# Output mixing on four row groups, with a signal per half of four pictures and corrections read by 16 transfers a wave

## Chip, cores and metric

The kernel runs on one core of a Trainium2 chip. The metric is the time on the device in microseconds (us). The kernel before took 838.54 us, the median of three runs (838.18 to 841.1).

## What is computed

The input is a batch of 32 pictures with 64 channels and 32 x 32 pixels. A first part (group normalization, windowed attention and a feed-forward layer) gives a new `x`. A second part, the one this case is about, adds a correction to it:

```python
# scores of 16 blocks of 8x8 positions, softmax, the 6 best positions, their features, then a small MLP
h = jax.nn.relu(feat @ W1 + b1)
rec = (h @ W2 + b2).reshape(NB, n, OC, LH, LW)
grid = rec.reshape(LRF, LRF, n, OC, LH, LW).transpose(2, 3, 0, 4, 1, 5)
grid = grid.reshape(n, OC, H, W)
return jnp.einsum('bohw,co->bchw', grid, out_w)
...
x = x + _L1_conv_ref(_gn(x), ...)
```

There are NB = 16 blocks of 64 positions in a picture, n = 32 pictures and OC = 7 reduced channels. So `rec` holds 512 rows (block and picture) of 7 x 64 = 448 numbers. The last line, the output mixing, turns the 7 reduced channels of each pixel into 64 channels by a 64 x 7 matrix, and the result is added to `x`. All numbers are float32.

## The kernel before

SBUF holds the pictures as 16 pairs: partitions 0 to 63 are the channels of picture p, partitions 64 to 127 those of picture 16 + p, and a pair has 1024 pixels in its free dimension. `xs` is the normalized `x` (its space is free once the features are picked), `x1` is the `x` to which the correction is added. Everything here happens in the last stage of the program. Each engine has a list of instructions written out by hand, and semaphores set the order between them.

The steps of the tail, with their lines:

- L1592: TensorE computes the second layer of the MLP for four tiles of 128 rows, in the order 0, 2, 1, 3 (`ROW_TILES`), into banks 4 to 7 of PSUM. L1490: VectorE adds the bias of each and writes `rec`, in SBUF.
- L1407: SP, whose queue issues the transfers, stores each tile of `rec` to a scratch tensor in DRAM. The trip through DRAM turns rows of blocks and pictures into rows of channels.
- L1414: after every second tile (tiles 0 and 2 are the first eight pairs of both image halves, tiles 1 and 3 the last eight), SP waits until both stores have landed and issues two reads. Read a (for the pictures of half a) fills the 7 partitions from 7a on: 14 partitions in all, 8 pairs x 1024 pixels each, in runs of 64 numbers. This is called a wave here; there are two waves, h = 0 and 1.
- L1601: TensorE mixes. For each pair and each half of its pixels (512, one bank of PSUM) it waits until the bank is free and forms two products of 256 columns. The weights `ow` are 128 x 128: rows 0 to 6 hold the mixing matrix for the picture of partitions 0 to 63, rows 7 to 13 the one for the other picture, and the other 114 rows are zero. Only banks 0 and 1 are used. Each product runs as two passes in float32.
- L1496: VectorE adds the bank (128 x 512) to `x1` and signals. There are 32 such adds.
- L1422: SP waits for both adds of a pair and issues two stores of 64 partitions x 4 KB each to the output, 32 in all.
- L1324: earlier, one stage before, SP loads the weights of this stage, `ow` with two loads.

Order and waits: TensorE's half of a pair waits for the add of the same half of the pair before; VectorE waits for each half's products; SP issues the stores of `rec`, the reads and the output stores in this order in one queue. ACT's queue has no transfers in this stage, and ScalarE's last work in it is the first layer's activation (L1531). `after(eng, sem, count)` is a wait that is left out where the count is not positive.

## Time and profile before

| | us |
|---|---|
| median of three runs | 838.54 |
| profiled execution, its whole time | 839.52 |
| span of that execution, first to last instruction | 837.7 |
| TensorE matmul busy in the span | 718.8 |
| VectorE busy in the span | 518.8 |
| last matmul of the MLP to the end of the span, about | 51 |

The span is the stretch that the traces show; what lies outside it (839.52 - 837.7 = 1.8 us) is not broken down. Busy time of an engine counts its instructions only, not its waits. The changed part is the last 51 us or so: from 787 us, when TensorE finishes the MLP, to 837.7 us, when the last store has landed. In tables by stage, the granted clock is given as a share of TensorE's 2.4 GHz, so 1.00 is 2.4 GHz and 0.50 is 1.2 GHz. The DMA share is the mean busy share of 16 DMA engines by the times of their packets; packets can overlap, so it can pass 1.

### The profile page before, as it was taken

The page shows a single profiled execution, that of the slowest core. Times are in us where ns is not written, and L with a number is a line of the kernel's source. Part 1 is how long each engine was busy: PE and PEld are TensorE (multiplying, and loading weights), DVE is VectorE, ACT ScalarE, POOL GpSimd, SP SyncE. Part 2 cuts the span into 40 slices and gives each one's busy share as a digit, 9 for nine tenths or more (in the row PEclk, how much of TensorE's full clock was granted, in tenths as well). Part 3 has the DMA queues.
Part 4 walks back from the last instruction along what each step waited for, and adds up shares of the span by engine and source line. Part 5 has one row for each costly group of instructions (what it writes and reads, how often), then busy time and mean ns, then how long its engine had stood idle before and what let it go on. Part 6 is the DMA issues. An engine that isn't in the chain of part 4 may idle for free. (4 is left out here: it accounts for less than half of the span.)

```text
span 837.7 us, 21571 instructions
## 1 busy us (share of the span) xinstructions
PE 718.8 (86%) x8482; PEld 385.6 (46%) x8482; DVE 518.8 (62%) x964; ACT 488.4 (58%) x986; POOL 373.9 (45%) x464
## 2 busy tenths in 40 slices
PE   4784799999999999999998489999999648659587
PEld 3562455555555555555554132333333228644264
DVE  4791367767776676777776112777777857661155
ACT  3663366777777777777775368877777117733000
POOL 4696356677767677667766220022222233300000
PEclk9775599999999999999999879999999758969889
DMA  9630000000000000000000020221111212000478
GB/s 211 149 87 11 1 2 2 2 3 2 2 2 3 2 3 3 2 2 2 3 2 3 0 51 1 49 50 46 45 43 49 76 43 54 0 1 1 57 165 268
DMA packets 15436, 31.38 MB, mean 37 GB/s; under 512 B 7208, under 2 KB 9004, under 8 KB 15340
## 3 DMA queue, kind: packets, MB, share of 16 engines
q1 hardware_dynamic: 14216, 29.61, 14.5%
q8 instruction: 66, 1.08, 0.6%
q10 hardware_dynamic: 856, 0.20, 0.2%
q0 software_dynamic: 272, 0.27, 0.2%
q14 instruction: 26, 0.21, 0.1%
HBM read 20.70 MB, written 9.37 MB: 36 GB/s over the span
## 5 line engine op out<-in xcount | busy, mean ns | idle before, releaser
L757 POOL TENSOR_TENSOR sc<-sc,mx 128x512 f32<-128x512 f32 x128 | 133.6, 1044 | 34.2 <-DVE mx L705 34.2
L702 DVE TENSOR_TENSOR sc<-s_ps,bias_tab 128x512 f32<-128x512 f32 x128 | 87.7, 685 | 58.9 <-PE s_ps L532 58.9
L655 ACT ACTIVATE pt<-t_ps 128x512 f32<-128x512 f32 x128 | 75.9, 593 | 52.6 <-PE t_ps L543 51.4
L1199 POOL TENSOR_TENSOR square<-xs 128x1024 f32<-128x1024 f32 x16 | 33.8, 2110 | 162.2 <-DVE xs L1101 162.2
L705 DVE TENSOR_REDUCE mx<-sc 128x8 f32<-128x512 f32 x128 | 87.8, 686 | 4.4
L1018 ACT ACTIVATE hs<-h_ps,fb1s 128x512 f32<-128x512 f32 x128 | 78.1, 688 | 17.6 <-PE h_ps L932 17.5
L543 PEld LDWEIGHTS t_ps<-consts,sc 128*128 128x128 f32 x512 | 53.7, 141 | 73.1 <-issue 45.8
L543 PE MATMUL t_ps<-consts,sc 128*128 128x128 f32 x512 | 83.9, 286 | 2.2 <-ACT pt L655 1.6
L532 PE MATMUL s_ps<-kx,qu 32*64 32x128 f32 x2048 | 71.4, 276 | 1.5 <-DVE sc L702 1.4
L932 PE MATMUL h_ps<-xs,fw 64*128 64x512 f32 x256 | 68.4, 648 | 1.0 <-ACT hs L1018 1.0
L945 PE MATMUL c_ps<-hs,fw 128*64 128x512 f32 x256 | 62.0, 604 | 0.8 <-DVE fcsq L1045 0.7
L532 PEld LDWEIGHTS s_ps<-kx,qu 32*64 32x64 f32 x2048 | 56.0, 133 | 13.8 <-issue 12.0
L646 ACT ACTIVATE vd<-a_ps 64x256 f32<-64x256 f32 x128 | 48.2, 377 | 18.4 <-PE a_ps L485 17.3
L742 POOL TENSOR_TENSOR q_sq<-q_sb 128x512 f32<-128x512 f32 x32 | 33.2, 1039 | 48.7 <-ACT q_sb L622 48.7
L713 DVE TENSOR_TENSOR kx<-a_ps,k_sb 128x512 f32<-128x512 f32 x64 | 40.9, 681 | 22.4 <-PE b_ps L509 21.4
L728 DVE TENSOR_TENSOR ob<-b_ps,rsum 128x512 f32<-128x512 f32 x32 | 22.1, 692 | 48.3 <-ACT rsum L664 48.3
L1045 DVE SCALAR_TENSOR_TENSOR fcsq<-c_ps,fb,fcc 128x512 f32<-128x512 f32 x32 | 23.8, 745 | 39.7 <-ACT fcc L1027 39.7
L764 POOL TENSOR_TENSOR cc<-xs,cc 128x512 f32<-128x512 f32 x32 | 40.7, 1275 | 13.9 <-DVE cc L734 13.9
L145 POOL TENSOR_TENSOR xs<-raw,gn_rstd_sb 128x96 f32<-128x96 f32 (+1 forms) x144 | 37.6, 306 | 18.7 <-ACT bias_ps L198 10.7
L742 POOL TENSOR_TENSOR k_sq<-k_sb 128x512 f32<-128x512 f32 x32 | 33.2, 1040 | 25.9 <-ACT k_sb L615 25.9
L1601 PE MATMUL bank<-xs,ow 128*128 (+1 forms) x128 | 34.6, 417 | 11.0 <-DMA xs<-rec_scratch 11.0
L749 POOL TENSOR_TENSOR csq<-cc 128x512 f32<-128x512 f32 x32 | 33.3, 1039 | 20.7 <-ACT cc L671 20.7
(190 smaller groups left out, 1393.2 us busy)
## 6 DMA issues: line engine op xcount, KB each, us to landing
raw<-in_x_dram SPq DMA_DIRECT2D x32, 256.0 KB, 5.1
xr<-in_x_dram SPq DMA_DIRECT2D x32, 256.0 KB, 4.1
out_dram<-x SPq DMA_DIRECT2D x32, 256.0 KB, 3.8
rec_scratch<-r SPq DMA_DIRECT2D x4, 224.0 KB, 4.5
xs<-rec_scratch SPq DMA_DIRECT2D x4, 224.0 KB
w<-in_L_conv_W_dram SPq DMA_DIRECT2D x1, 784.0 KB
w<-in_L_conv_W_dram SPq DMA_DIRECT2D x1, 672.0 KB
consts<-in_c_consts_dram SPq DMA_DIRECT2D x1, 400.0 KB, 4.0
```

The lines of the kernel that those rows point to most:

```text
L532: last = pe.matmul(s_ps[j][TOK * w:TOK * (w + 1), 2 * i + m], qu[p % 2][a][row, at], kx[p % 2][a][row, :, at], start=True, stop=True)
L543: last = pe.transpose(t_ps[:, m], sc[n % KEPT][:, m].rearrange("c h k -> c (h k)"), ident)
L646: last = act.activation(to[to_lo:to_hi, :, w, :, DH * h:DH * (h + 1)], v[lo:hi, :, :, h], ACT.Copy)
L655: act.activation(pt[a][2 * hp + j][:, :, :], t_ps[:, :, :], ACT.Exp).then_inc(s["exped"], 1)
L702: dve.tensor_tensor(sc[n % KEPT][:, :, :, :], s_ps[j][:, :, :, :], bias_tab[:, j, hp], ALU.add)\
L705: dve.tensor_reduce(mx[n % KEPT][:, :], sc[n % KEPT][:, :, :, :].rearrange("c m h k -> c (m h) k"), X, ALU.max).then_inc(s["row_max"], 1)
L713: dve.tensor_tensor(kx[p % 2][a][:, h], a_ps[a][:, :], k_sb[a][:, :], ALU.mult)\
L742: pool.tensor_tensor(dst[a][:, :], src[a][:, :], src[a][:, :], ALU.mult).then_inc(s[done], 1)
L757: pool.tensor_tensor(v, v, mx[n % KEPT][:, :].unsqueeze(2).broadcast_to([128, 8, TOK]), ALU.subtract)\
L932: last = pe.matmul(h_ps[2 * half + a][:, :], fw1[lo:hi, a, half], xu[lo:hi, u], start=True, stop=True)
L945: last = pe.matmul(c_ps[lo:hi, :], fw2[:, m // 2], hs[:, u % 2, m], start=(m < 2), stop=(m >= 2))
L1018: act.activation(hs[:, u % 2, m], h_ps[m][:, :], ACT.Gelu, bias=fb1s[:, m // 2:m // 2 + 1])\
```

## The change

The mixing is laid over the four groups of 32 rows of the TensorE array. Pair p = 4k + q uses row group q: its 14 rows of corrections lie at partitions 32q to 32q + 13, in slot k of a `grid` that now has four slots of 1024 pixels for each row group (the first four pair slots of `xs`). `ow` gets a copy of the mixing matrix in each group. A call of `mix(k, half)` forms eight products, for four pairs and two quarters of 256 columns, with q innermost, so neighbouring products have different row groups and different banks; all eight banks are used, bank 2q + half for half a picture pair. It signals once for the eight products, and VectorE makes four adds behind each signal. A pair is stored after its second half, so SP waits for add number 8(p // 4) + p % 4 + 5. The reads of a wave become 16 transfers, eight (image half 0) from SP and eight (image half 1) from ACT, each for one q and one k. TensorE additionally waits until VectorE has read banks 4 to 7 (`rec`). The loops of the mixing, the adds and the stores are written out.

```diff
--- before.py
+++ after.py
@@ -1264,7 +1264,8 @@
                       (w2[:, :, :], mlp_w2.rearrange("(m k) n -> k m n", k=MT)), (mb[:, :], mlp_b1),
                       (mb2r[:, :], mlp_b2.rearrange("(a n) -> a n", a=1).broadcast_to([128, OUTDIM]))]
         for a, (lo, hi) in enumerate(HALVES):
-            tail_loads += [(w1s[lo:hi, :], mlp_w1[TOP * C:INDIM]), (ow[OC * a:OC * (a + 1), lo:hi], out_w)]
+            tail_loads += [(w1s[lo:hi, :], mlp_w1[TOP * C:INDIM])]
+            tail_loads += [(ow[32 * q + OC * a:32 * q + OC * (a + 1), lo:hi], out_w) for q in range(4)]
 
         with ExitStack() as stage:
             s = {k: sem(stage, "y_" + k) for k in
@@ -1376,7 +1377,7 @@
 
             rec = r[:, :, :, :].rearrange("c t n x -> c (t n x)")[:, 0:4 * OUTDIM].rearrange("c (t n) -> c t n", t=4)
 
-            grid = yt.rearrange("o p g n -> o p (g n)")
+            grid = xs[:, 0:4]
             psb = [ps(stage, f"bank{k}", [128, COLS]) for k in range(8)]
             ROW_TILES = (0, 2, 1, 3)
 
@@ -1398,6 +1399,17 @@
                                 src[:, :, :, :, q, a])
                 return last
 
+            def spread_rec(eng, h, a):
+
+                eng.wait_ge(rec_out[h], 32)
+                rows = rec_dram[256 * a + 128 * h:256 * a + 128 * (h + 1)]
+                for q in range(4):
+                    first = 32 * q + OC * a
+                    src = rows.rearrange("(k q g) (o l) -> q o k g l", k=2, q=4, l=TOK)[q]
+                    dst = grid[first:first + OC, 2 * h:2 * h + 2].rearrange("o k (g l) -> o k g l", l=TOK)
+                    for k in range(2):
+                        eng.dma_start(dst[:, k], src[:, k]).then_inc(rec_in[h], 16)
+
             with nc.Block() as block:
                 @block.sync
                 def _(sp):
@@ -1405,23 +1417,15 @@
                     for i, t in enumerate(ROW_TILES):
                         sp.wait_ge(s["rec"], i + 1)
                         sp.dma_start(rec_dram[128 * t:128 * (t + 1), :], rec[:, t]).then_inc(rec_out[i // 2], 16)
-                        if i % 2 == 0:
-                            continue
-                        h = i // 2
-                        sp.wait_ge(rec_out[h], 32)
-                        for a in range(2):
-                            rows = slice(256 * a + 128 * h, 256 * a + 128 * (h + 1))
-                            sp.dma_start(grid[OC * a:OC * (a + 1), 8 * h:8 * (h + 1)]
-                                         .rearrange("o p (g l) -> o (p g) l", l=TOK),
-                                         rec_dram[rows].rearrange("r (o l) -> o r l", l=TOK)).then_inc(rec_in[h], 16)
+                        if i % 2 == 1:
+                            spread_rec(sp, i // 2, 0)
                     out_pairs = out.rearrange("(a p) c h w -> a c p (h w)", a=2)
 
                     def store(p):
-                        sp.wait_ge(s["added"], 2 * p + 2)
+                        sp.wait_ge(s["added"], 8 * (p // 4) + p % 4 + 5)
                         for a, (lo, hi) in enumerate(HALVES):
                             sp.dma_start(out_pairs[a, :, p], x1[lo:hi, p]).then_inc(s["stored"], 16)
-                    store(0)
-                    with sp.Fori(1, PAIRS) as p:
+                    for p in range(PAIRS):
                         store(p)
                     sp.wait_ge(s["stored"], 32 * PAIRS)
 
@@ -1489,16 +1493,12 @@
                         dve.wait_ge(s["rec_ps"], i + 1)
                         dve.tensor_tensor(rec[:, t], psb[4 + i][:, 0:OUTDIM], mb2r[:, :], ALU.add).then_inc(s["rec"], 1)
 
-                    def add(p):
+                    for k in range(4):
                         for half in range(2):
-                            dve.wait_ge(s["mixed"], 2 * p + half + 1)
-                            v = x1[:, p, COLS * half:COLS * (half + 1)]
-                            dve.tensor_tensor(v, v, psb[half][:, :], ALU.add).then_inc(s["added"], 1)
-                    add(0)
-                    add(1)
-                    with dve.Fori(1, PAIRS // 2) as i:
-                        add(2 * i)
-                        add(2 * i + 1)
+                            dve.wait_ge(s["mixed"], 2 * k + half + 1)
+                            for q in range(4):
+                                v = x1[:, 4 * k + q, COLS * half:COLS * (half + 1)]
+                                dve.tensor_tensor(v, v, psb[2 * q + half][:, :], ALU.add).then_inc(s["added"], 1)
 
                 @block.scalar
                 def _(act):
@@ -1529,6 +1529,8 @@
                     for m in range(4):
                         act.wait_ge(s["hid_ps"], m + 1)
                         act.activation(hid[:, m], psb[m][0:MT, :], ACT.Relu, bias=mb[:, m:m + 1]).then_inc(s["hid"], 1)
+                    for h in range(2):
+                        spread_rec(act, h, 1)
 
                 @block.tensor
                 def _(pe):
@@ -1593,21 +1595,21 @@
                                              start=(m == 0), stop=(m == 3))
                         last.then_inc(s["rec_ps"], 1)
 
-                    def mix(p):
+                    def mix(k, half):
+                        after(pe, s["added"], 8 * (k - 1) + 4 * (half + 1))
+                        for y in range(2):
+                            for q in range(4):
+                                rows = slice(32 * q, 32 * q + 2 * OC)
+                                blk = grid[rows, k].rearrange("o (y x h w) -> o y h x w", y=4, x=4, h=8)[:, 2 * half + y]
+                                last = pe.matmul(psb[2 * q + half][:, 256 * y:256 * (y + 1)], ow[rows, :], blk,
+                                                 start=True, stop=True)
+                        last.then_inc(s["mixed"], 1)
+                    pe.wait_ge(s["rec"], len(ROW_TILES))
+                    for k in range(4):
+                        if k % 2 == 0:
+                            pe.wait_ge(rec_in[k // 2], 256)
                         for half in range(2):
-                            after(pe, s["added"], 2 * p - 1 + half)
-                            for y in range(2):
-                                blk = grid[:, p].rearrange("o (y x h w) -> o y h x w", y=4, x=4, h=8)[:, 2 * half + y]
-                                last = pe.matmul(psb[half][:, 256 * y:256 * (y + 1)], ow[:, :], blk,
-                                                 start=True, stop=True)
-                            last.then_inc(s["mixed"], 1)
-                    for h in range(2):
-                        pe.wait_ge(rec_in[h], 32)
-                        mix(8 * h)
-                        mix(8 * h + 1)
-                        with pe.Fori(4 * h + 1, 4 * (h + 1)) as i:
-                            mix(2 * i)
-                            mix(2 * i + 1)
+                            mix(k, half)
 
 
 N_PICK = 13
```

## Rows read from the trace of the kernel before

**Rows 1.** Chain that ended last, 770 to 838 us: start, length, what.

```profile
781.67 1.94 DMA rec_scratch<-r
...
783.97 13.96 DMA xs<-rec_scratch
...
797.97 34.63 PE bank L1601 x128
...
832.74 0.69 DVE x L1496
```

**Rows 2.** Who waited for whom, same stretch: total us, times, longest.

```profile
PE bank L1601 <- DMA xs<-rec_scratch: 11.0, 1, 11.0
```

**Rows 3.** VectorE: the adds as a group, first add, two adjoining instructions elsewhere.

```profile
L1496 DVE TENSOR_TENSOR x<-x,bank 128x512 f32 (+1 forms) x32 | 22.0, 687 | 23.8 <-PE bank L1601 23.8
...
800.08 0.69 DVE L1496 TENSOR_TENSOR x<-x,bank 128x512 f32<-128x512 f32 x1 [12.43 <-PE bank L1601]
...
518.77 0.75 DVE L1045 SCALAR_TENSOR_TENSOR fcsq<-c_ps,fb,fcc 128x512 f32<-128x512 f32 x1 [2.61 <-ACT fcc L1027]
519.44 0.74 DVE L1061 SCALAR_TENSOR_TENSOR fcc<-fcc,b,xs 128x512 f32<-128x512 f32 x1
```

**Rows 4.** Stages: length, busy of five engines (x count), PEclk, DMA share, GB/s.

```profile
784.50:785.50 1.00, 1.00 (x4) 0.55 (x3) 0.15 (x1) 0.00 (x0) 0.00 (x0) 1.00 0.32 75
785.50:791.50 6.00, 1.49 (x4) 0.40 (x3) 0.62 (x1) 0.00 (x0) 0.00 (x0) 0.96 0.63 34
...
793.00:796.50 3.50, 0.00 (x0) 0.00 (x0) 0.00 (x0) 0.00 (x0) 0.00 (x0) 0.50 0.66 47
...
799.50:800.50 1.00, 1.00 (x4) 0.81 (x3) 0.42 (x1) 0.00 (x0) 0.00 (x0) 0.50 0.44 98
800.50:805.00 4.50, 4.50 (x18) 3.23 (x18) 2.78 (x5) 0.00 (x0) 0.00 (x0) 0.92 0.62 39
805.00:812.00 7.00, 7.00 (x28) 4.42 (x27) 4.47 (x8) 0.00 (x0) 0.00 (x0) 1.00 1.07 191
812.00:824.00 12.00, 12.00 (x48) 7.84 (x46) 8.10 (x12) 0.00 (x0) 0.00 (x0) 1.00 0.92 334
824.00:832.00 8.00, 8.00 (x32) 5.23 (x31) 5.10 (x9) 0.00 (x0) 0.00 (x0) 1.00 0.86 249
```

**Rows 5.** Packets of the stretch 775 to 838 us, and its transfers by name.

```profile
DMA packets 6749, 10.24 MB, mean 163 GB/s; under 512 B 4188, under 2 KB 4700, under 8 KB 6748
...
out_dram<-x SPq DMA_DIRECT2D x32, 256.0 KB, 3.8
rec_scratch<-r SPq DMA_DIRECT2D x4, 224.0 KB, 4.5
xs<-rec_scratch SPq DMA_DIRECT2D x4, 224.0 KB
```

**Rows 6.** TensorE at 199 us: start, busy, products on four row groups.

```profile
199.32 0.70 PE L507 MATMUL a_ps<-rn,spread_keys 32*128 32x512 f32 x2 [0.31 <-ACT rn L635]
199.34 0.70 PE L509 MATMUL b_ps<-rn,consts 32*128 32x512 f32 x2
199.86 0.59 PE L507 MATMUL a_ps<-rn,spread_keys 32*128 32x512 f32 x2
199.87 0.59 PE L509 MATMUL b_ps<-rn,consts 32*128 32x512 f32 x2
```

**Rows 7.** Issue on SP: ns min/median/max, first and last start; a held issue; the second wave.

```profile
L1414 SPq DMA_DIRECT2D xs<-rec_scratch x4: 292/630/1052, 783.6 to 798.9; - x4
...
L1422 SPq DMA_DIRECT2D out_dram<-x x32: 494/495/2362, 802.3 to 834.3; - x32
...
784.97 6.37 SPq L1407 DMA_DIRECT2D rec_scratch<-r  x1
...
798.54 1.39 SPq L1414 DMA_DIRECT2D xs<-rec_scratch  x2
```

**Rows 8.** Loads of the mixing weights, and VectorE's first instruction of the stage.

```profile
L1324 SPq DMA_DIRECT2D ow<-in_L_conv_out_w_dram x2: 479/507/535, 689.9 to 691.0; - x2
...
727.93 0.59 DVE L1438 COPY scores_sb<-raw_scores 64x256 f32<-64x256 f32 x2 [3.19 <-PEq L1319]
```

## The prediction: what the change does to the time

> **What bounds the kernel now.** I read the chain of waits of the last stretch first, then who waited for whom, then the timeline of the queues, and last the busy time and the transfer rate by stage. The chain [rows 1] shows two long pieces after the second layer of the MLP. From 783.97 to 797.93 us nothing computes: TensorE waits 11.0 us for the corrections to come back from DRAM [rows 2]. From 797.97 the 128 matmul passes of the output mixing (64 products, two passes each) run 34.63 us to 832.60, and one add and the last store close the span at 837.7. So two things hold the tail: how long the first wave of read-back takes, and TensorE's pace in the mixing, 34.63/16 = 2.16 us a picture pair.
>
> Two resources lie close beneath TensorE. VectorE's 32 adds take 22.0 us in all [rows 3], about two thirds of the mixing. The transfers are nearer. The reader should look at the last two columns of the stage table [rows 4]: share of the 16 DMA engines and GB/s. The reads of corrections move 75 and 98 GB/s in their first microsecond, and then only 34, 47 and 39 GB/s, although the share stays above 0.6. From 812 to 824 us the stores run at 334 GB/s, and only from 824 at 249, which is TensorE's pace (a pair is 524 KB; 524/2.16 = 243). The time between is a backlog being worked off.
>
> Why reads are so slow can be half read from packet counts. Each read takes 256-byte runs (64 floats); four reads are 4 x 7 x 128 = 3584 packets. The stretch has 4188 packets under 512 bytes [rows 5]. The 604 left over are completions: 32 stores x 16, 4 stores of `rec` x 16 and 4 reads x 7 make 604 exactly. So a read runs on 7 of the 16 engines, as it has 7 channel rows outermost, and the other 9 do none of it. Each new transfer has 7 rows outermost too, so I count on 7 again. The Trainium skill has a rule for this in "DMA: Bandwidth & Descriptors" (Why a DMA increments its semaphore by 16 and not by 1): the slowest dimension of the two patterns sets the number of engines, and the trace agrees with its 604.
>
> In the fast first microsecond 7 engines at 75 to 98 GB/s do a run in 256 x 7/98 to 256 x 7/75 = 18 to 24 ns each; later at 34 to 47 GB/s one in 38 to 53 ns. So an engine can take runs twice as fast as it mostly does, and something behind it holds it. What the trace does not show is what.
>
> **Part by part.** *The mixing on four row groups.* A product now has 14 rows of weights at partition 32q, and neighbours lie on different groups and write different banks. The trace has that very pattern in another stage: four products of 512 columns on row groups 0 to 3 (the two of L507, the two of L509), two passes each, start at 199.32 and end at 200.46 us [rows 6]: 1.14 us for all four. One call of the new `mix(k, half)` has four groups with 2 x 256 columns each, the same columns, so 1.14 us at full clock instead of 4 x 1.08 us. At half clock I take 2.11 us, the time from the first pass at 797.97 [rows 1] to the first add at 800.08 [rows 3], where two 256-column products ran one after the other at clock 0.50 [rows 4]. Both ends lie under the 4 x 0.69 = 2.76 us that the adds of such a half need, and banks of one half are refilled while the other half is added. So TensorE leaves the path; what is late next is VectorE, then the transfers.
>
> *The adds.* Still 32 of 687 ns. Where two such instructions had no wait between them they started 0.67 us apart [rows 3]; 32 x 0.69 = 22.0 us. A signal now stands for four adds: the first add waits for eight products instead of two. If the groups overlap fully this costs nothing at the start (2.11 us both ways); at the trace's other end, no overlap, 4 x 2.11. I take nothing, by the nearest row [rows 6].
>
> *The stores.* The first one waits for five adds, 5 x 0.69 = 3.4 us after the first add starts, not two. Within a group of four pairs nothing is stored for 2.8 us and then a pair every 0.69 us. Two stores of 0.495 us issue time each [rows 7] make 0.99 us a pair on SP, so a burst of four is issued in 4.0 us, inside the 5.5 us that a group's adds take. That costs at most 1.2 us at the very end.
>
> *The reads, issue.* A wave of 2 transfers becomes 16, eight on SP, eight on ACT, which has no work behind. By 0.292 to 0.495 us an issue [rows 7] this is 2.3 to 4.0 us on each queue. On SP, the two later stores of `rec` queue behind it, and in the second wave the output stores. At present the third store of `rec` is held at issue from 784.97 for 6.37 us anyway [rows 7], and no output store is ready before the adds are, so neither pays. The completions of a wave rise from 14 to 112; output stores have one completion for every four 4 KB packets and still move 334 GB/s, so I take nothing. The upper bound is one drain a transfer; that is a rival below.
>
> *The reads, pace.* Bytes, run length and engines stay: 458,752 bytes a wave, 256 runs an engine. What changes is that the two image halves travel at the same time on two queues, and that the partitions written are spread over four groups of 32 instead of 14 neighbours. Bounds from rows: the slow pace of before, 34 to 47 GB/s (a wave in 14 us), and the fast start, 98 GB/s (4.7 us). Each engine of before wrote one single partition row for 128 runs on end. I hold that the slow phase is back-pressure of the writes (fast until something is full, then slow with the engines' share unchanged at 0.6), and that two destinations at once take twice 39 GB/s, about 75: 6.1 us, and with 0.9 us from issue to the first packet and 0.4 us of completion 7.4 us. But this is the term that I know least.
>
> *The weights of the mixing.* `ow` gets eight small loads instead of two, six more of 0.51 us of issue on SP at about 691 us, 3.1 us in all, and VectorE first asks for these loads after 727.93 us [rows 8]. The stage between, 36 us, hides them; without it they would cost 3.1 us. Unrolled loops of adds and stores cost nothing that a row shows.
>
> **The sum**, in the span of the profiled run. First wave issued at 783.6, landed 791.2. The stores of `rec` sit behind SP's reads and land about 1 us later, 792.3 (before, the second wave is issued at 798.54 [rows 7], 0.6 us after the first landed at 797.93). Second wave issued 792.3, landed 799.9. First add 791.2 + 2.1 = 793.3; first 16 adds to 804.3, when the second wave has long landed; last add ends 793.3 + 22.0 = 815.3. First store 793.3 + 3.4 = 796.7. The stores are 8.39 MB. Engines 0 to 6 carry 7/16 of that, 3.67 MB, and are held by reads until 799.9. In 812 to 824 the nine others, which had no backlog, moved 9/16 x 249 = 140 GB/s, so the seven moved 334 - 140 = 194: 3.67 MB take 18.9 us, to 818.8. All sixteen together: the highest stretch is 334 GB/s, which gives 25.1 us, to 821.8; should the whole array do what the seven show (28 GB/s an engine) VectorE's 815.3 and the seven bind instead. I take 821.8. Behind it the last store's completion: before, the last issue starts at 834.3 [rows 7] and the span ends 3.4 us later, of which 0.5 is issue and 0.6 the packets; 2.3 us remain. End 824.1. Outside the span lie 839.52 - 837.7 = 1.8 us, and the profiled run was 1.0 us above the median of the runs: 824.1 + 1.8 - 1.0 = 824.9, say 825.
>
> **The rivals.** *Reads no faster (0.33).* The cause of the slow pace is in the seven engines or in DRAM, and two queues share it. For it: the share of the engines is the same 0.6 at 34 and at 39 GB/s. Against: the fast first microsecond. Then the first wave lands at 798, adds run from 800.1 to 811.1, the second wave ends at about 811 as before (458,752 bytes: 98 KB to 800.5, then 39 GB/s), second adds to 822.5, and the seven engines start on their 3.67 MB only at 811: 829.9, plus 2.3 is 832.2, plus 0.8 is 833.0. The Trainium skill states this outcome as a rule ("DMA: Bandwidth & Descriptors", Issuing engines are not separate DMA queues): transfers issued from several engines run on the same 16 and only issue time is saved. No row of this trace has two queues reading small runs side by side, so it neither bears this out nor refutes it.
>
> *Row groups do not overlap in this form (0.06).* The mixing keeps its 34.6 us from 791.3 on, end 791.3 + 34.6 + 5.1 = 831.0, time 831.8; together with the first rival 838. Against it stand the four products of another stage [rows 6], on the same 32 x 128 tiles.
>
> *Completions drain the queues (0.08), the slower side.* If each transfer's completion must wait for its writes before the next one's runs go on, a queue loses one write latency a transfer. From rows, the shortest store of `rec` takes 1.94 us from issue to landing [rows 1], of which some 1 us is waiting. Eight in a row on each queue are 8 us a wave, 16 us in the two waves. On top of the first rival this gives 833.0 + 16 = 849; on top of doubled reads, 841. It passes the time of before once the two waves together take 5.5 us longer than now. Against it: output stores with a completion after every fourth packet of an engine at full pace.
>
> **How the numbers follow.** Forecast 825, chance 0.53, its own range 819 (reads at 98 GB/s throughout, stores bound by VectorE and 28 GB/s an engine) to 829 (reads 1.3 times as fast as now). Rivals 0.33, 0.06, 0.08. Half a per cent, 4.2 us, is about what a measurement of this kernel tells from no change. Faster by more: the forecast, two thirds of the first rival (833.0 lies just below the 834.3 that is needed) and most of the second, 0.79. Within: the rest of these, 0.14. Slower: the third rival, 0.07. The range runs from 819 to 835, which leaves out the slower side and some of the first rival.
>
> **What would show it.** In the trace after: TensorE's wait for the corrections of 4 to 5 us instead of 11.0; the transfer rate in the first wave near 75 GB/s past its first microsecond; VectorE with 16 adds about 0.69 us apart and a busy share near 1 in the mixing; `mix` calls of 1.1 to 2.1 us; the span ending 6 to 9 us after the last add, held by stores and not by products. Wrong would be: a rate again at 34 to 47 GB/s in both waves (first rival); gaps in the adds that TensorE ends (second); a rate that falls to near nothing between transfers, or SP still issuing reads when adds are done (third).

## The result and the profile after

The changed kernel takes 830.5 us (median of four runs, 828.9 to 832.1) beside 838.4 us for the kernel before on the same chip: a ratio of 0.990, 95% interval 0.987 to 0.993, faster by 7.9 us. The forecast was 825, faster by 13.5. The profiled execution has a span of 829.9 us.

The chain that ended last, and below it who waited for whom (total us, times, longest), to be set beside [rows 1] and [rows 2]:

```profile
781.71 1.93 DMA rec_scratch<-r
...
786.33 4.81 DMA xs<-rec_scratch
...
791.27 2.12 PE bank L1604 x16
...
793.42 16.83 DVE x L1501 x28
810.24 0.60 DVEq L1413
...
DVE x L1501 <- PE bank L1604: 5.7, 1, 5.7
...
PE bank L1604 <- DMA xs<-rec_scratch: 4.2, 1, 4.2
```

The first wave is issued at 783.67 us. It lands in time for TensorE's first product at 791.27, 7.6 us later, where it took 14.3 us before. The adds then run without a gap that TensorE ends: the 5.7 us that VectorE waits for a product is one wait, at the start. The chain by itself ends with VectorE's adds near 812.6 us. The span goes on for 17.3 us, and the chain view does not say why. The rates do. Columns as in [rows 4]:

```profile
784.50:785.50 1.00, 1.00 (x4) 0.51 (x3) 0.19 (x1) 0.00 (x0) 0.00 (x0) 1.00 0.39 88
785.50:787.50 2.00, 1.54 (x5) 0.44 (x3) 0.42 (x1) 0.00 (x0) 0.00 (x0) 1.00 0.52 102
793.00:794.00 1.00, 1.00 (x14) 0.87 (x14) 0.58 (x1) 0.00 (x0) 0.00 (x0) 0.50 0.50 110
794.00:797.50 3.50, 2.61 (x28) 1.55 (x20) 3.50 (x7) 0.00 (x0) 0.00 (x0) 0.50 0.59 85
799.50:813.00 13.50, 9.29 (x76) 5.16 (x68) 13.13 (x22) 0.00 (x0) 0.00 (x0) 0.50 0.82 266
813.00:826.00 13.00, 0.00 (x0) 0.00 (x0) 0.00 (x0) 0.00 (x0) 0.00 (x0) 0.50 0.83 278
```

The reads now hold 85 to 102 GB/s past their first microsecond, against 34 to 47 before. The stores, from 799.5 to 826, run at 266 and 278 GB/s, while VectorE is at work and also after it has finished. Before, there was a stretch of 334. The queues, the adds and a mixing call in order of time, then the issue times and the packets of ACT's queue:

```profile
791.70 2.94 SPq L1411 DMA_DIRECT2D xs<-rec_scratch  x8
796.52 29.91 SPq L1427 DMA_DIRECT2D out_dram<-x  x32
...
793.42 19.22 DVE L1501 TENSOR_TENSOR x<-x,bank 128x512 f32<-128x512 f32 x32 [5.72 <-PE bank L1604]
...
798.35 2.09 PE L1604 MATMUL bank<-xs,ow 14*128 14x256 f32 x16 [0.30 <-DVE x L1501]
...
L1427 SPq DMA_DIRECT2D out_dram<-x x32: 516/867/1367, 796.5 to 825.8; - x32
...
L1411 SPq DMA_DIRECT2D xs<-rec_scratch x16: 288/324/395, 783.7 to 794.3; - x16
L1411 ACTq DMA_DIRECT2D xs<-rec_scratch x16: 273/346/401, 783.7 to 794.6; - x16
...
q10 hardware_dynamic: 1904, 0.46, 4.1%
```

Here the reader should see three things. The adds are 19.22 us for 32, 0.60 us apart. A mixing call of eight products (16 passes) takes 2.09 us at the half clock: TensorE sits idle for 4.2 us before the first call, and PEclk reads 0.50 in every stretch shown from 793 us on. From the second call on this costs nothing, since the adds set the pace; the first call is on the chain, 2.15 us from the first product at 791.27 to the first add at 793.42 (the run by_slot_2q below shows what it takes at the full clock). And issuing an output store takes 0.867 us in the median instead of 0.495 [rows 7]. I read this as SP being held back by stores that have not gone out. ACT's queue carries 1904 packets: 2 x 7 x 128 runs and 16 x 7 completions, so each new read again uses 7 engines.

The parts of the program before 783 us shift by up to 8 us from one profile to another with the same instructions. So below, each kernel is also measured by its own tail: from the issue of the first read of the profiled execution to the end of its span. Each tail is that of one profile; three profiles with the same reads and stores (changed, changed again, neighbours in one row group) gave 46.2, 46.0 and 45.9 us.

| kernel | median, us | ratio to before (95%) | first wave, us | tail, us |
|---|---|---|---|---|
| before | 838.4 | | 14.3 | 54.1 |
| changed | 830.5 | 0.990 (0.987 to 0.993) | 7.6 | 46.2 |
| changed, again beside the last two | 832.2 | 0.989 (0.985 to 0.992) | 8.0 | 46.0 |
| reads on SP alone | 838.5 | 0.998 (0.995 to 1.000) | 12.4 | 52.3 |
| before, reads on two queues | 835.0 | 0.994 (0.991 to 0.997) | 9.0 | 49.6 |
| neighbours in one row group | 831.1 | 0.990 (0.987 to 0.993) | 7.6 | 45.9 |
| stores on two queues | 827.1 | 0.984 (0.979 to 0.988) | 7.9 | 41.2 |
| stores of two pairs | 829.7 | 0.988 (0.983 to 0.992) | 8.1 | 43.6 |
| two queues and two pairs | 827.4 | 0.985 (0.982 to 0.988) | 7.8 | 43.4 |
| stores of four pairs | 835.4 | 0.994 (0.992 to 0.996) | 8.1 | 50.0 |
| stores grouped by half | 839.2 | 0.999 (0.997 to 1.001) | 7.9 | 52.3 |
| two queues in the same half | 837.0 | 0.997 (0.995 to 0.999) | 7.7 | 50.7 |
| two queues, reads by slot | 823.4 | 0.979 (0.977 to 0.982) | 4.7 (half a wave) | 38.1 |
| two queues, reads merged | 827.5 | 0.983 (0.980 to 0.986) | 9.4 | 42.1 |

The ratio is to the kernel before measured beside it, whose median was 838.4 for the changed kernel and 839.6 to 840.7 for the others. The first wave is from its first issue to the first product.

### The profile page after: what moved, and what is told of

The parts are those of the page before. It is cut to its first block and busy times, and to the rows that moved or that the text cites. A ratio compares the mean times of both kernels' runs of the same rounds, so it can differ in the third digit from the quotient of the medians.

```text
span 829.9 us, 21353 instructions
## 1 busy us (share of the span) xinstructions
PE 699.6 (84%) x8482; PEld 371.9 (45%) x8482; DVE 516.4 (62%) x964; ACT 488.6 (59%) x986; POOL 374.4 (45%) x464
## 3 DMA queue, kind: packets, MB, share of 16 engines
q1 hardware_dynamic: 12592, 29.16, 13.2%
## 5 line engine op out<-in xcount | busy, mean ns | idle before, releaser
L543 PEld LDWEIGHTS t_ps<-consts,sc 128*128 128x128 f32 x512 | 53.7, 141 | 73.1 <-issue 45.9
L485 PEld LDWEIGHTS a_ps<-wv,xs 128*128 128x128 f32 x256 | 33.0, 209 | 17.9 <-ACT k_sb L615 17.9
```

The lines of the kernel that those rows point to most:

```text
L543: last = pe.transpose(t_ps[:, m], sc[n % KEPT][:, m].rearrange("c h k -> c (h k)"), ident)
```

## The experiments

Two questions are to be settled: what made the reads faster (two queues, or the spread over partitions and small transfers), and why the stores run at 270 GB/s and not at 334.

### The reads: one queue or two

**reads_on_sp.** The changed kernel, with all 16 transfers of a wave on SP:

```diff
                         if i % 2 == 1:
                             spread_rec(sp, i // 2, 0)
+                            spread_rec(sp, i // 2, 1)
...
-                    for h in range(2):
-                        spread_rec(act, h, 1)
```

> The changed kernel with one thing undone: all 16 read-back transfers of a wave are issued by SP, none by ACT. Theory 'two queues make the reads fast': a wave again takes about 12 to 14 us from issue to landing (it takes 7.5 us with two queues), the first product starts near 797 us instead of 791.3, and the time goes up by 5 to 10 us, to 836 to 840. Theory 'spread partitions make the reads fast': the wave is held only by the issue of 16 transfers at 0.35 us, 5.6 us, instead of 2.8; the first product starts near 793 and the time rises by 1 to 4 us.

Measured: 838.5 us, first wave 12.4 us. The queue, the adds and the stages:

```profile
784.37 6.19 SPq L1411 DMA_DIRECT2D xs<-rec_scratch  x16
...
797.65 6.04 SPq L1411 DMA_DIRECT2D xs<-rec_scratch  x16
...
798.96 9.65 DVE L1502 TENSOR_TENSOR x<-x,bank 128x512 f32<-128x512 f32 x16 [10.56 <-PE bank L1603]
...
787.00:791.00 4.00, 0.73 (x2) 0.01 (x1) 0.62 (x1) 0.00 (x0) 0.00 (x0) 1.00 0.62 42
800.00:804.00 4.00, 2.81 (x28) 1.33 (x20) 4.00 (x8) 0.00 (x0) 0.00 (x0) 0.50 0.62 40
```

The reads are back at 42 and 40 GB/s in spite of their new shape and their spread over four groups of partitions. Issue takes 6.2 us, so it is not the bound of 12.4. Also to be seen: the first 16 adds take 9.65 us and then wait for the second wave. So with reads on one queue the fast mixing and the new shape of the reads are together worth 1.8 us of the tail (54.1 to 52.3) and no more.

**before_two_queues.** The kernel before, with the read of picture half 1 issued by ACT:

```diff
-                        for a in range(2):
-                            rows = slice(256 * a + 128 * h, 256 * a + 128 * (h + 1))
-                            sp.dma_start(grid[OC * a:OC * (a + 1), 8 * h:8 * (h + 1)]
...
+                        read_back(sp, h, 0)
...
+                    for h in range(2):
+                        act.wait_ge(rec_out[h], 32)
+                        read_back(act, h, 1)
```

> The kernel before with one thing of the change: the read of picture half 1 of each wave is issued by ACT instead of SP, still one transfer of 7 x 128 runs into 7 neighbouring partitions. Theory 'two queues': the wave lands near 791 us instead of 797.9, the mixing (34.6 us, still bound by TensorE) starts 6 to 7 us earlier and so the time falls by 6 to 7 us, to about 832. Theory 'spread partitions': the wave still lands near 797 and the time stays at 838.

Measured: 835.0 us, ratio 0.994. The queue, the first products and the stages:

```profile
780.49 0.30 SPq L1403 DMA_DIRECT2D xs<-rec_scratch  x1
...
789.45 6.30 PE bank L1606 x16
...
786.00:788.00 2.00, 0.00 (x0) 0.00 (x0) 0.00 (x0) 0.00 (x0) 0.00 (x0) 0.97 0.60 86
793.00:795.00 2.00, 2.00 (x7) 1.60 (x6) 0.77 (x2) 0.00 (x0) 0.00 (x0) 0.57 0.61 78
```

Two large transfers into 14 neighbouring partitions, at 86 and 78 GB/s: the wave takes 9.0 us instead of 14.3. The two runs together say which part of the change made the reads fast. The second queue takes 5.4 us off a wave of the old shape and 4.8 us off one of the new; the new shape takes 1.9 us off on one queue and about 1.4 on two. Of the 6.7 us by which the first wave is shorter, the second queue is most. They do not say why. The second queue always carried the other picture half: other partitions and another region of the scratch tensor. So whether a queue holds the pace at 34 to 47 GB/s, or a single stream of reads into one set of seven partitions does, is not shown; a run with two queues on the same picture half would tell. The tail did not get 6 to 7 us shorter as expected, but 4.5: the mixing starts 5.4 us sooner and, still bound by TensorE, is itself 0.9 us longer (789.45 to 824.96, 35.5 us). From these 49.6 us to the 46.2 of the changed kernel the mixing on row groups, with the new shape of the reads, takes off another 3.4.

### The order of the products

**same_group.** The changed kernel, with the two products of a row group as neighbours:

```diff
-                        for y in range(2):
-                            for q in range(4):
+                        for q in range(4):
+                            for y in range(2):
```

> The changed kernel with the two inner loops of a mix call exchanged: the two products of one row group are neighbours. Theory 'the row groups are off the path': products overlap only at the change of group, a call takes 5 slots instead of 2 (2.65 us at full clock, 5.3 us at half clock). If the busier TensorE is granted the full clock, the last add moves from 812.6 to about 816, under the stores' end at 829, and the time stays within 1.5 us. If it stays at half clock, adds pace at 5.3 us a call, the last one at 836, and the time rises by 8 us or more.

Measured: 831.1 us. One mixing call, and the adds:

```profile
799.47 2.11 PE L1604 MATMUL bank<-xs,ow 14*128 14x256 f32 x16 [0.28 <-DVE x L1501]
...
794.55 19.24 DVE L1501 TENSOR_TENSOR x<-x,bank 128x512 f32<-128x512 f32 x32 [5.67 <-PE bank L1604]
```

A call takes 2.11 us instead of 2.09, at the same half clock, and not the five slots that I had counted. The four row groups are kept busy in either order. So it is the use of four groups that counts here, and neighbouring products on different groups bring 0.02 us a call. Since the call hardly changed, this run does not test whether a slower TensorE would show in the time.

### The stores: halves, queue or chip

In the changed kernel transfers of half 0 (partitions 0 to 63) and half 1 (64 to 127) take turns in one queue. Three theories: both halves must be in flight together; a queue limits or pays for each transfer; 270 GB/s is the limit of the chip.

**stores_two_queues.** Half 0 on SP, half 1 on ACT:

```diff
...
                     for p in range(PAIRS):
-                        store(p)
+                        ready(sp, p)
+                        store(sp, p, 0)
...
+                    for p in range(PAIRS):
+                        ready(act, p)
+                        store(act, p, 1)
```

> The changed kernel with the output stores of picture half 1 issued by ACT, those of half 0 by SP. Theory 'halves' (a transfer of 64 partitions reaches only part of the ways out of SBUF, and all 16 engines work on the same transfer at once, so both halves must be in flight together): the stores run at 330 GB/s or more instead of 270 and the time falls by 5 us or more, to 825. Theory 'queue' (a queue holds only some four transfers in flight; 4.1 us from issue to landing over 0.93 us between issues is 4.4): the same fall, since there are two queues. Theory 'chip' (270 GB/s is what sixteen engines write to DRAM): no change, within 1 us.

Measured: 827.1 us, tail 41.2 instead of 46.2.

```profile
805.00:815.00 10.00, 8.79 (x72) 4.98 (x64) 10.00 (x18) 0.00 (x0) 0.00 (x0) 0.50 0.98 342
815.00:827.00 12.00, 0.04 (x4) 0.00 (x0) 2.68 (x5) 0.00 (x0) 0.00 (x0) 0.50 0.95 333
```

342 and 333 GB/s: 'chip' falls, and 'halves' and 'queue' both stand. It also shows that the stores, and nothing before them, held the end of the changed kernel.

**stores_two_pairs.** One transfer for two pairs, one queue:

```diff
...
+                    for p in range(0, PAIRS, 2):
+                        ready(sp, p + 1)
                         for a, (lo, hi) in enumerate(HALVES):
-                            sp.dma_start(out_pairs[a, :, p], x1[lo:hi, p]).then_inc(s["stored"], 16)
+                            sp.dma_start(out_pairs[a, :, p:p + 2], x1[lo:hi, p:p + 2]).then_inc(s["stored"], 16)
```

> The changed kernel with one output transfer for two pairs of a picture half (64 partitions x 2 x 4 KB), 16 transfers of 512 KB instead of 32 of 256 KB, issued in the same queue. Theory 'queue': twice the bytes are in flight, the rate rises above 330 GB/s, and the time falls by 3 us or more although the first store waits for one add more. Theory 'halves': each transfer still covers one half of the partitions for longer, so the rate stays at 270 or falls, and the time stays or rises by 1 to 2 us. Theory 'chip': the rate stays, plus 0.7 us.

Measured: 829.7 us, tail 43.6.

```profile
803.00:813.00 10.00, 6.45 (x52) 3.65 (x48) 9.91 (x17) 0.00 (x0) 0.00 (x0) 0.50 0.99 325
813.00:825.00 12.00, 0.00 (x0) 0.00 (x0) 0.00 (x0) 0.00 (x0) 0.00 (x0) 0.50 0.99 330
```

The rate rises to 325 and 330 GB/s, as 'queue' had it and 'halves' had not. From the two periods (0.97 us for 256 KB, 1.57 us for 512 KB) I formed a new theory, a gap of 0.38 us for each transfer, and put it to three tests.

**stores_2q_2p.** Both remedies at once:

```diff
...
+                    for p in range(0, PAIRS, 2):
+                        ready(sp, p + 1)
+                        store2(sp, p, 2, 0)
...
+                    for p in range(0, PAIRS, 2):
+                        ready(act, p + 1)
+                        store2(act, p, 2, 1)
```

> The changed kernel with two pairs in each output transfer and with picture half 1 stored by ACT, half 0 by SP: 8 transfers of 512 KB on each queue. Theory 'each transfer costs its queue a gap': with a period of 0.97 us for 256 KB (270 GB/s) and 1.57 us for 512 KB (334 GB/s) on one queue, a 4 KB packet of an engine takes 0.148 us and a transfer costs 0.38 us beside it. Both remedies at once then gain over either only if no common limit stands at 335 to 345 GB/s. Without such a limit the stores pass 380 GB/s and the time falls to about 823; with it ('chip' limit, now at 340 instead of 270) the rate stays at 340 and the time is that of the better of the two, 827, within 1.5 us.

Measured: 827.4 us, tail 43.4.

```profile
802.00:811.00 9.00, 5.97 (x48) 3.37 (x45) 9.00 (x16) 0.00 (x0) 0.00 (x0) 0.50 1.00 326
812.00:820.00 8.00, 0.00 (x0) 0.00 (x0) 0.00 (x0) 0.00 (x0) 0.00 (x0) 0.50 1.02 385
820.00:825.40 5.40, 0.00 (x0) 0.00 (x0) 0.00 (x0) 0.00 (x0) 0.00 (x0) 0.50 0.46 168
```

The time is the 827 that a common limit at 340 had been expected to give, but the rate is not: it is 326 until 811, then 385 GB/s, so there is no such limit. What the higher rate gains is lost at both ends. From 800 to 802 the rate is still only 254, and the last 5.4 us run at 168, the last of them nearly empty. That some engines finish early, with eight large transfers a queue, would explain the end; it is argued, not seen.

**stores_four_pairs.** One transfer of 1 MB for four pairs, one queue:

```diff
...
+                    for p in range(0, PAIRS, 4):
+                        ready(sp, p + 3)
+                        for a in range(2):
+                            store2(sp, p, 4, a)
```

> The changed kernel with one output transfer for four pairs of a picture half (1 MB, 16 packets of 4 KB an engine), 8 transfers on SP. 'Gap per transfer': period 0.38 + 16 x 0.148 = 2.75 us, 382 GB/s, if nothing else limits; with a common limit 335 to 345. Both start three adds later. The time is 828 to 831. 'Halves': under 270 GB/s and above 832.

Measured: 835.4 us, tail 50.0: the time is on the side of 'halves'.

```profile
802.00:806.00 4.00, 3.40 (x32) 2.02 (x28) 4.00 (x8) 0.00 (x0) 0.00 (x0) 0.50 0.95 200
822.00:829.00 7.00, 0.00 (x0) 0.00 (x0) 0.00 (x0) 0.00 (x0) 0.00 (x0) 0.50 1.00 342
```

From 802 to 806, when the engines should all be in the first transfer, of one half (1 MB at 200 GB/s takes 5.2 us), the rate is 200 GB/s with the engines' share at 0.95; later, with several transfers queued, it is 342. The gap theory has no place for the 200, and 'halves' in its plain form none for the 342 of one queue.

**stores_grouped.** The same 32 transfers on SP in another order, four of half 0, then four of half 1:

```diff
...
+                    for k in range(PAIRS // 4):
+                        for a in range(2):
+                            for q in range(4):
+                                ready(sp, 4 * k + q)
+                                store(sp, 4 * k + q, a)
```

> The changed kernel with the same 32 output transfers on SP in another order: for each four pairs first the four of picture half 0, then the four of half 1. 'Gap per transfer': order plays no part, 270 GB/s again, the time within 2 us of the changed kernel's. 'Halves': runs of 1 MB from one half of the partitions slow the stores to 220 GB/s or less, and the time rises by 5 us or more.

Measured: 839.2 us, tail 52.3.

```profile
799.00:803.00 4.00, 3.60 (x32) 2.43 (x32) 4.00 (x8) 0.00 (x0) 0.00 (x0) 0.50 0.97 204
799.00:834.00 35.00, 10.36 (x80) 6.08 (x80) 14.21 (x24) 0.00 (x0) 0.00 (x0) 0.50 0.93 229
```

Same number of transfers, same size, same queue; the order alone takes the rate from 270 to 229, with plateaus at 204. The gap theory falls.

**stores_2q_same_half.** Two queues, but both in the same half at a time:

```diff
...
+                    for k in range(PAIRS // 4):
+                        for a in range(2):
+                            for q in (0, 2):
+                                ready(sp, 4 * k + q)
+                                store(sp, 4 * k + q, a)
...
+                    for k in range(PAIRS // 4):
+                        for a in range(2):
+                            for q in (1, 3):
+                                ready(act, 4 * k + q)
+                                store(act, 4 * k + q, a)
```

> The changed kernel with its output stores on two queues, SP the even pairs and ACT the odd ones, and for each four pairs first the transfers of picture half 0 on both queues, then those of half 1: two queues as in stores_two_queues, but both mostly in the same half of the partitions. Theory 'halves': the second queue brings nothing, the stores run at 200 to 230 GB/s, 52 us from the first read issue to the end, time 838. Theory 'a queue has a gap for each transfer': two queues cover each other's gaps, 330 GB/s as in stores_two_queues, 41 to 43 us, time 827 to 829.

Measured: 837.0 us, tail 50.7.

```profile
802.00:805.00 3.00, 2.40 (x24) 1.35 (x20) 3.00 (x6) 0.00 (x0) 0.00 (x0) 0.50 0.96 206
802.00:834.00 32.00, 8.62 (x68) 4.95 (x64) 12.47 (x21) 0.00 (x0) 0.00 (x0) 0.50 0.96 243
```

243 GB/s over all, and 206 in the first microseconds, while both queues are in one half. The second queue that brought 5 us brings 1.6 here (tail 50.7 beside the 52.3 of stores_grouped). So what counts is that both halves are in flight: 200 to 206 GB/s from one, up to 385 from two. One reservation: half of the partitions is also half of the pictures, and so another region of the output in DRAM. Whether the limit lies at the SBUF side or at the DRAM side these runs can't say. The Trainium skill puts it at the SBUF side ("SBUF — State Buffer", Door 1: The DMA port swizzle): 64 partitions on one side reach 8 of 16 ports, about 218 GB/s. The plateaus measured here, 200 to 206, lie just under that. The same page of the Trainium skill says ("Can I just issue two DMAs to hit both halves?") that two transfers on the two halves serialize and gain only 6% over a single one. Here both halves on two queues run at 333 to 342 GB/s beside 200 to 206 for one half at a time, and the measurement decides.

What stays open is why transfers of two pairs on one queue reach 330. A reading that fits all rows is that engines drift apart when each has eight packets queued in a transfer, so that some are in one half and some in the other; no view of the profile shows single engines, so this is only argued.

### Towards a better version

**by_slot_2q.** stores_two_queues, with the reads ordered by slot and a semaphore for each slot, so that TensorE starts on the first four pairs after half a wave:

```diff
-                for q in range(4):
...
-                    for k in range(2):
-                        eng.dma_start(dst[:, k], src[:, k]).then_inc(rec_in[h], 16)
+                for k in range(2):
+                    for q in range(4):
...
+                        eng.dma_start(dst[:, k], src[:, k]).then_inc(rec_in[2 * h + k], 16)
...
-                        if k % 2 == 0:
-                            pe.wait_ge(rec_in[k // 2], 256)
+                        pe.wait_ge(rec_in[k], 128)
```

> The changed kernel with its output stores on two queues (as stores_two_queues) and the read-back transfers of a wave ordered by slot: first the four row groups of slot k, with a semaphore of their own for each slot, then those of slot k + 1. TensorE starts on the first four pairs when half the wave has landed. If the head start counts (stores set the end, from the first one on): first product 5 us after the wave's issue instead of 7.6, stretch from the first read issue to the end 39 us instead of 41.2, time 825. If the engines that carry the second wave set the end, the head start is lost: 41 us, 827.

Measured: 823.4 us, ratio 0.979 to the kernel before, tail 38.1: the fastest of all. The first two calls, the chain from the first call on, the stage in which they run, the queue of SP, and the stages of the stores:

```profile
787.59 2.01 PE L1611 MATMUL bank<-xs,ow 14*128 14x256 f32 x32 [1.34 <-DMA xs<-rec_scratch]
...
787.59 1.18 PE bank L1611 x16
...
788.79 11.45 DVE x L1505 x19
...
788.00:789.00 1.00, 1.00 (x26) 1.00 (x22) 0.21 (x1) 0.00 (x0) 0.00 (x0) 1.00 0.75 228
...
790.44 2.94 SPq L1420 DMA_DIRECT2D xs<-rec_scratch  x8
793.42 21.84 SPq L1406 DMA_DIRECT2D out_dram<-x  x16
...
796.00:808.00 12.00, 8.36 (x64) 5.05 (x64) 12.00 (x21) 0.00 (x0) 0.00 (x0) 0.50 1.01 359
808.00:819.00 11.00, 0.00 (x0) 0.00 (x0) 0.01 (x1) 0.00 (x0) 0.00 (x0) 0.50 0.99 345
```

The first product starts 4.7 us after the wave's issue at 782.89, and the stores, which begin at 793.42, hold 345 to 359 GB/s to the end. Measured from the first read issue and set beside stores_two_queues, the first product comes 3.2 us sooner, the first store 2.6 (10.5 against 13.2 us), and the end 3.1: the head start arrives at the end, since the stores are the bound from the first on. Two more things can be read here. TensorE has been idle for only 1.3 us when its data come and still has the full clock (PEclk 1.00), so the first call takes 1.18 us before the first add, not the 2.12 of the changed kernel: about 1 us of the head start is the clock. And the first store could have come sooner. Five adds are done at about 791.9 us (788.79 + 4 x 0.60 + 0.68), but SP is issuing the reads of the second wave from 790.44 to 793.38, and the store is issued at 793.42. So in this kernel the issue of the reads has come onto the path, for 1.5 us.

**merged_2q.** stores_two_queues, with pairs numbered so that a row group needs one transfer instead of two:

```diff
-                    for k in range(2):
-                        eng.dma_start(dst[:, k], src[:, k]).then_inc(rec_in[h], 16)
+                    eng.dma_start(dst, src).then_inc(rec_in[h], 16)
```

> The changed kernel with stores on two queues, and the pairs numbered so that both slots of a row group come in one transfer: 4 transfers of 7 x 32 runs on each queue and wave instead of 8 of 7 x 16. 'Issue holds the reads': four issues of 0.35 us less, the wave lands in 6.2 us instead of 7.6. 'The seven engines hold them': the same 458,752 bytes at 80 to 100 GB/s, the wave takes 7.2 us or more. Time 825 to 827.

Measured: 827.5 us, tail 42.1. SP's issues and the first products:

```profile
784.77 1.51 SPq L1422 DMA_DIRECT2D xs<-rec_scratch  x4
...
794.20 3.80 PE L1613 MATMUL bank<-xs,ow 14*128 14x256 f32 x32 [6.06 <-DMA xs<-rec_scratch]
```

The issues take 1.5 us instead of 2.9, but the wave takes 9.4 us instead of 7.9. Issue does not hold the reads; that fewer and longer transfers are slower by 1.5 us I had not expected, and it agrees with the 1.4 us between the old shape and the new on two queues. It is seen in one profile of each, and its cause is not shown: with fewer issues before them, the stores of `rec` also go out sooner here (1.6 us after the first read instead of 2.9), and they share the engines with the reads.

**after_again** is the changed kernel beside these two:

> The changed kernel itself, on the chip of these runs, as a measure for the two beside it: about 831, and 46 us from the first read issue to the end.

Measured: 832.2 us, tail 46.0. As expected.

## Why the prediction was right in its mechanism and too high in its gain

*Reads.* The step "two destinations at once take twice 39 GB/s" gave the right number: forecast 791.2 us for the first product's data, measured 791.27; the second wave was issued at 791.70, forecast 792.3. That it is right to 0.1 us is partly luck. The terms named (6.1 + 0.9 + 0.4 = 7.4 us from 783.6) make 791.0, not 791.2. And the reads did not hold 75 GB/s: until 787 they ran at 91 in the mean, and the other half of their bytes, some 230 KB, took until about 790.9 at some 60 GB/s, beside the 459 KB of the last two stores of `rec`, for which the forecast took nothing. (These shares are worked out from rates of half a microsecond and the known bytes.) The reason was tested in part. I had named the two queues and the spread over partitions together and leaned on the writes. The runs show that the spread and the small transfers are a minor part (1.9 and 1.4 us) and the second queue the larger (5.4 and 4.8); that two destinations at once are what helps is neither shown nor refuted, since no run had the one without the other. The first rival (reads no faster, 0.33) fell in the first rows of the trace after. The rule of the Trainium skill beside it ("DMA: Bandwidth & Descriptors", Issuing engines are not separate DMA queues), that a second issuing engine saves issue time only, does not hold for these reads: in the old shape issue was two instructions, and the wave still went from 14.3 to 9.0 us.

*Mixing.* Forecast 2.11 us a call at half clock, measured 2.09; first add forecast 793.3, measured 793.42. The second rival fell. That TensorE leaves the path behind its first call is shown by the chain, in which 28 adds follow each other, and by the adds' single wait for a product. At the full clock, the first two calls of by_slot_2q took 2.01 us together, near the 1.14 us each that was taken from [rows 6].

*Adds.* Forecast 22.0 us, measured 19.22, since queued adds start 0.60 us apart instead of 0.69. Only the first five are on the path, before the first store; the rest gained nothing.

*First store.* Forecast 796.7, measured 796.52.

*Stores.* This is the step that failed: "All sixteen together: the highest stretch is 334 GB/s, which gives 25.1 us". Measured 266 to 278 GB/s; 8.39 MB from 796.5 to 829 are 258 GB/s over all, 32.5 us. So the stores took 7.4 us longer than forecast. With 2.3 us behind them I had the end at 824.1; no bytes move after 829, so only 0.9 us lay behind, which gave 1.4 us back, and the first store was 0.2 us early. The end came at 829.9, and these 5.8 us are the whole of the miss (5.5 in the medians, 830.5 against 825). One sign on record failed with it: the span was to end 6 to 9 us after the last add, and ended 17.3 after it. The row of 334 was read rightly as a backlog of the seven engines, but its meaning was turned round. I took it for a low bound of what sixteen engines do, when it was a high one: there seven engines lagged behind nine, so two groups worked on different transfers and, by the experiments on the halves, likely on different halves. In the changed kernel all sixteen go through the same transfers in step. This account of the 334 is argued from the runs on the halves; no view shows which engine works on which transfer. My price for the seven engines (28 GB/s each, 18.9 us) never came into play.

*Completions.* The third rival (completions drain the queues) did not come about: reads with 112 completions a wave are faster than reads with 14.

*Issue, weights, the unrolled loops.* As forecast nothing: issue of eight reads took 2.86 us (2.3 to 4.0 forecast), hidden on the way to the landing of the wave. No run tested the weights or the loops by themselves.

## What to carry to other kernels

When an engine is taken off the path, ask of the resource behind it not only how fast it has been seen to run, but in what pattern it ran then; a stretch worked off by part of the engines is another pattern than a steady stream. Small reads from DRAM are worth trying on two queues at once, and large stores so that both halves of the partitions (here also both halves of the output) are in flight together: here that is 270 against 338 GB/s for one more list of instructions. Where transfers bound the end, each microsecond by which the first of them starts earlier is a microsecond gained: by_slot_2q got it by letting the products start after half a wave of reads. Once such a start comes early, look at what else stands in the queue before the first store.

## What was not expected of the hardware

- One queue took reads of 256-byte runs at 34 to 47 GB/s in both shapes, after a faster first microsecond (75 and 98); two queues, each with its own picture half, took them at 78 to 102, again on seven engines for each transfer.
- Stores from one half of the partitions (and to one half of the output) run at 200 to 206 GB/s, alternating in one queue at 266 to 278, on two queues at 333 to 342, in large transfers up to 385.
- Eight products on four row groups of 32 take 2.09 us with neighbours on different groups and 2.11 with neighbours on the same group, both at the half clock; at the full clock two such calls took 2.01 us.
- Adds of 128 x 512 out of PSUM, each 0.678 us long, start 0.60 us apart when none has to wait.
- Reads of 7 x 32 runs took 1.5 us longer for a wave than twice as many of 7 x 16, in one profile of each.
